# A recurrent vision tower with experts: the token embedding in row halves, its bias added by GpSimd, and another order of the first steps

## The reference

```python
h = patches(x) @ W.T + b                              # 16 x 784 x 64
xp = layernorm(h) @ W_ih.T + b_ih + b_hh
for t in range(16):                                   # the images are the time steps
    hid = tanh(xp[t] + hid @ W_hh.T)
    h2[t] = h[t] + hid
x = layernorm(h2)
top2 = top_k(x @ gate_w + gate_b, 2); w = softmax(top2)
moe = sum over the two of w * (relu(x @ w1[e] + b1[e]) @ w2[e] + b2[e])   # 16 experts, F = 128
y = x + moe
out = h2 + layernorm(y) * gamma + beta
```

## Time and profile before

| | us |
|---|---|
| median of 3 runs | 524.08 |
| the runs | 524.26, 524.08, 521.48 |
| the profiled execution, its own time | 524.21 |
| its span, first to last instruction | 522.4 |
| PE busy | 498.9 (95%) |
| DVE busy | 440.8 (84%) |
| ACT busy | 343.6 (66%) |
| POOL busy | 176.9 (34%) |
| DMA queue q1, share of 16 engines | 56.3% |

### The profile page before, as it was taken

The page is one execution under the profiler, slowest core; times in us unless marked ns, Lnnn a source line. Parts: engine busy times, 40 slices in busy tenths (PEclk is TensorE's granted clock), DMA queues, the critical chain, the costliest instruction groups (busy, mean ns, idle before and its releaser), DMA issues.

```text
span 522.4 us, 8674 instructions
## 1 busy us (share of the span) xinstructions
PE 498.9 (95%) x2943; PEld 331.1 (63%) x2943; DVE 440.8 (84%) x873; ACT 343.6 (66%) x592; POOL 176.9 (34%) x126
## 2 busy tenths in 40 slices
PE   4788999999999999999999999999999999999993
PEld 4464666666666767666666666667666667656552
DVE  1656796998989899898989899898989979999775
ACT  3545575757768585766858576675858577665652
POOL 4220111613325262533425262323516243313233
PEclk9998999999999999999999999999999999999997
DMA  6219076764829185573919377390948548392901
GB/s 139 75 45 232 31 165 140 171 150 109 194 62 230 54 194 124 130 172 85 234 28 221 97 154 168 89 212 25 218 100 181 125 95 193 97 209 65 221 20 32
DMA packets 29755, 69.04 MB, mean 132 GB/s; under 512 B 6432, under 2 KB 8464, under 8 KB 29584
## 3 DMA queue, kind: packets, MB, share of 16 engines
q1 hardware_dynamic: 29712, 68.49, 56.3%
HBM read 60.39 MB, written 8.08 MB: 131 GB/s over the span
## 4 chain that ended last, share of the span: by engine, by line
PE 89%; issue 3%; POOL 3%; DMA 2%; DVE 2%; ACT 1%; POOLq 0%; SPq 0%; DVEq 0%; ACTq 0%
PE pZ L865 37%; PE pO L881 35%; PE pA L780 3%; PE pA L816 2%; PE pA L834 2%; PE pA L895 2%; PE pB L780 2%; PE pA L804 2%; DMA spread<-gates_dram 1%; POOL inv_std L354 1%; PE pB L846 1%; PE pA L792 1%; PE pB L895 1%; PE pB L834 1%; PE pA L805 1%
## 5 line engine op out<-in xcount | busy, mean ns | idle before, releaser
L480 ACT ACTIVATE hexp<-pZ,b1c 128x784 f32<-128x784 f32 x256 | 221.4, 911 | 107.2 <-PE pZ L865 107.2
L881 PE MATMUL pO<-hexp,w2s 128*64 128x392 f32 x1024 | 199.8, 506 | 0.6 <-ACT hexp L480 0.3
L865 PE MATMUL pZ<-xt,w1hi 128*128 128x392 f32 x512 | 189.4, 370 | 1.0 <-ACT xt L411 1.0
L648 DVE SCALAR_TENSOR_TENSOR prod<-pO,b2c,spread 128x392 f32<-128x392 f32 x256 | 150.2, 621 | 44.1 <-PE pO L881 39.5
L865 PE MATMUL pZ<-xt,w1lo 128*128 128x392 f32 x512 | 175.9, 344 | 0.0
L354 POOL TENSOR_TENSOR inv_std<-var,nhalf 112x7 f32<-112x7 f32 x48 | 81.5, 1706 | 183.3 <-DVE var L549 183.3
L865 PEld LDWEIGHTS pZ<-xt,w1hi 128*128 128x128 f32 x512 | 97.3, 190 | 46.5 <-issue 26.3
L881 PEld LDWEIGHTS pO<-hexp,w2s 128*64 128x64 f32 x1024 | 70.5, 136 | 76.0 <-issue 64.9
L664 DVE TENSOR_TENSOR acc<-acc,prod 128x784 f32<-128x784 f32 x111 | 112.2, 1010 | 0.1
L865 PEld LDWEIGHTS pZ<-xt,w1lo 128*128 128x128 f32 x512 | 97.7, 191 | 0.0
L361 POOL TENSOR_TENSOR h2b<-h2c,bet 112x448 f32<-112x448 f32 x15 | 21.5, 1431 | 140.7 <-DMA h2c<-h_dram 140.7
(11 more groups left out here) (103 smaller groups left out, 482.8 us busy)
## 6 DMA issues: line engine op xcount, KB each, us to landing
spread<-gates_dram SPq DMA_DIRECT2D x128, 392.0 KB, 9.0
h_dram<-h SPq DMA_DIRECT2D x16, 248.1 KB, 2.4
h2c<-h_dram SPq DMA_DIRECT2D x16, 248.1 KB, 7.6
xcur<-x_in SPq DMA_DIRECT2D x16, 196.0 KB, 7.6
out<-yo SPq DMA_DIRECT2D x15, 196.0 KB, 7.2
w1f<-w SPq DMA_DIRECT2D x2, 512.0 KB, 6.0
w2s<-w SPq DMA_DIRECT2D x1, 512.0 KB, 3.7
gates_dram<-gt SPq DMA_DIRECT2D x16, 28.0 KB, 2.0
```

The costliest lines, as they stand in the source:

```text
L480: nc.scalar.activation(hexp[u % RING][:, :].rearrange("p (b c) -> p b c", b=2), halves(pZ[u % 2]), ACT.Relu, bias=b1c[:, u:u + 1]).then_in ...
L648: nc.vector.scalar_tensor_tensor(out=prod[q % RING][:, b * HALF:(b + 1) * HALF], in0=halves(pO)[:, b, :], scalar=b2c[:, q:q + 1], in1=spre ...
L865: last = nc.tensor.matmul(halves(pZ[e % 2])[:, b, :], w[:, e, :], xt[par][:, b * HALF:(b + 1) * HALF], start=(k == 0), stop=(k == 1))
L881: last = nc.tensor.matmul(halves(pO)[k * D:(k + 1) * D, b, :], w2s[:, e, :], hexp[e % RING][:, b * HALF:(b + 1) * HALF], start=True, stop= ...
```

## The change

Four things are changed.

1. The embedding. xcur becomes 128 partitions by 448: the even tiles' patches in partitions 0 to 63, the odd tiles' in 64 to 127 (the host orders x so). Each load of x is two transfers. tokw is held twice, once in each half, without the bias row, and embed_in takes rows 0 to 63 for even tiles and 64 to 127 for odd ones. The row of ones and its two fills by GpSimd go.
2. The bias. One more product in the fill makes tokb, the bias spread over 112 partitions, which VectorE copies. From step 3 on, keep_h1 still copies on ScalarE, and a new operation bias_h1 on GpSimd adds tokb in place, between add_beta and the MIX rstd in its queue; the square of h1 waits for it and moves from u = 11 (12 in step 0) to 13, its reduction on VectorE from u = 13 to 14. For steps 0 to 2 VectorE does copy and addition together.
3. Products on zeros: keep_busy(n) issues n products of 128 x 128 with 512 columns into a part of pO that nothing reads: 6 at the start, 9 behind embed_in(0), 4 behind recur(0), 10 ahead of x2_turn(0). VectorE fills their operand first.
4. The order of the fill and of step 0: embed_in(1) moves behind embed_turn(0), hidden_turn(0) ahead of embed_turn(1), gates_turn(0) ahead of first_layer(0, 0) and into another bank (pO), low_part(0) behind find_second(0), and w1's low parts, norms and squares of the first steps change places; in step 0 recur(2) is at u = 5, x2_turn(1) at 7, x2's scaling at 3 and low_part(1) at 5. The spread of step 0's gates is ten transfers instead of eight: the first pair alone, with a semaphore of its own.

The core of the diff:

```diff
-        tokw = sb("tokw", [K_IN + 1, W])
+        tokw = sb("tokw", [2 * D, W])
+        tokb = sb("tokb", [P, W])
-        xcur = [sb(f"xcur{i}", [K_IN + 1, TOK]) for i in range(2)]
+        xcur = [sb(f"xcur{i}", [2 * D, FIRST]) for i in range(2)]
...
+        def gates_turned_in(s):
+            return pO if known(s, 1) else pB
...
-                sp.dma_start(xcur[s % 2][0:K_IN, :], x_in[:, bass.ds(s * TOK, TOK)]).then_inc(xload[s % 2], 16)
+                for k, (first, n) in enumerate(((0, FIRST), (FIRST, REST))):
+                    sp.dma_start(xcur[s % 2][k * D:(k + 1) * D, 0:n],
+                                 x_in[:, bass.ds(s * TOK + first, n)]).then_inc(xload[s % 2], 16)
...
-                for part in range(PARTS):
+                pieces = [(part * (Q // PARTS), Q // PARTS, spread_in[part]) for part in range(PARTS)]
+                if known(s, 1):
+                    pieces[0:1] = [(0, 1, first_spread), (1, Q // PARTS - 1, spread_in[0])]
+                for q0, n, landed in pieces:
...
+            def bias_h1(s, par):
+
+                pool.wait_ge(h1_kept, 2 * s + 2)
+                nc.gpsimd.tensor_tensor(h1[par][:, :, :], h1[par][:, :, :], over_tiles(tokb[:, :], W), ALU.add)\
+                    .then_inc(h1_biased, 1)
...
                 if close:
                     add_beta(t - 1)
+                if embed:
+                    bias_h1(t + 3, 1 - par)
                 if mix:
                     rstd(MIX, t + 2, 1)
...
-                    if gate and u == at(t, 1, first=5):
+                    if gate and u == at(t, 1, first=7):
                         keep_xt(t + 1, 1 - par)
...
-                    if mix and u == at(t, 5, first=7):
+                    if mix and u == 5:
                         new_hidden(t + 2)
...
-                    if embed and u == at(t, 11, first=12):
+                    if embed and u == 13:
                         square_h1(t + 3, 1 - par)
...
+            def keep_h1(s, par):
+
+                dve.wait_ge(h1_made, s + 1)
+                if not known(s, 2):
+                    STATE.wait(dve, s - 2, "h2")
+                for some, n, fresh in zip(some_tiles, (PAIRS, TILES - PAIRS), embedded_in(s)):
+                    nc.vector.tensor_tensor(h1[par][:, some, :], fresh, tokb[:, :].unsqueeze(1).to_broadcast([P, n, W]),
+                                            ALU.add).then_inc(h1_kept, 1)
...
-                    if embed and u == 13:
+                    if embed and u == 14:
                         norm_var(EMBED, a, 0)
...
+            def keep_busy(n):
+
+                for _ in range(n):
+                    nc.tensor.matmul(pO[:, 512:1024], busy[:, 0:128], busy[:, :], start=True, stop=True)
...
-                    last = nc.tensor.matmul(embedded_in(s)[i % 2][:, i // 2, :], xcur[s % 2][:, i * P:(i + 1) * P],
-                                            tokw[:, :], start=True, stop=True)
+                    rows = slice((i % 2) * D, (i % 2 + 1) * D)
+                    last = nc.tensor.matmul(embedded_in(s)[i % 2][:, i // 2, :],
+                                            xcur[s % 2][rows, (i // 2) * P:(i // 2 + 1) * P], tokw[rows, :],
+                                            start=True, stop=True)
...
             embed_in(0)
-            embed_in(1)
+            keep_busy(9)
             pe.wait_ge(consts, IDENT_SET)
             embed_turn(0)
+            embed_in(1)
             pe.wait_ge(cell_loaded, CELL_LOADED)
             recur(0)
+            keep_busy(4)
+            hidden_turn(0)
             embed_turn(1)
-            hidden_turn(0)
             recur(1)
             embed_in(2)
...
+            keep_busy(10)
             x2_turn(0)
+            gates_turn(0, True)
             first_layer(0, 0, 0)
-            gates_turn(0, True)
             first_layer(0, 1, 0)
```

115 lines of the change are left out of this document (65 added, 50 removed).

## The result

The changed kernel took 517.29 us (median of 4 runs, 515.39 to 517.55), the kernel before 524.03 beside it: a ratio of 0.9875, 95% interval 0.9836 to 0.9913. That is 6.7 us or 1.25% less, more than the 0.5% that a measurement of this kernel can tell from no change. The forecast was 518.2, and the measured time lies in its own range (516.5 to 520.5). The profiled execution took 517.41 us, its span is 515.3.

A forecast was written before the change was run, and what follows sets the result against it. The prediction took TensorE, busy 60.00 of 60 us, to bound the kernel. 524.2 less 6.0 in the loop plus 0 for the fill gave 518.2 us, own range 516.5 to 520.5, 8 in 10 from 514.5 to 521.8.

The forecast's parts named there:

- Part 1: Loop, embed_in by row halves: a block takes 0.94 us instead of 1.40, 13 blocks, 6.0 us saved.
- The 9.1 us: Loop, embed_in: upper bound of the saving, if a block took half of 1.40 us; the sum would be 515.1.
- Part 2: Loop, bias on GpSimd: 2.2 us an operation, 0.8 us of VectorE, cost on the path 0.
- Part 3: Fill up to the first residual sum: VectorE waits for the expert weights, add_state(0) at about 22.5, 2.2 us late.
- Part 4: Fill, add_state(0) to gate copy: net 0.3 us worse, bounds -1.4 and +1.8; copy done at about 35.7.
- the 1.3: Fill, up to the gates: us gained by low_part, exp and gates_turn moving, if TensorE is free.
- Part 5: Fill, first pair spread alone: lands in 4.9 us, 2.9 us better; first product at 43.1.
- Part 6: Fill, first product to third pair: 7.6 us, reaching 50.7, plus 0.6 us for a possible cold clock.
- (a): Rival, fill: the zeros work, TensorE at full level at x2_turn(0) and after the pause; 515.5 us, chance 0.22.
- (b): Rival, fill loses: embed_in(1) and all zeros at half clock, the pause cold; 521.4 us, chance 0.15.
- (c): Rival, loop: halves don't overlap, or another engine takes up what TensorE gives; 524.2 us, chance 0.08.
- (d): Rival, loop: GpSimd's bias delays the next state's normalisation; at 1 us over, 531.2 us, chance 0.05.

The follow-up runs named there:

- e2: The changed kernel without GpSimd's addition of the bias to h1 from step 3 on: 516.45 us.
- e5: The changed kernel with SP's five expert weight loads issued ahead of the x loads of steps 2 and 3: 513.07 us.
- e3: The changed kernel without the ten zero products ahead of x2_turn(0): 515.57 us.
- e7: The changed kernel with the first spread in one piece of eight experts' pairs again: 520.69 us.
- e8: The kernel before with only the row halves, two x loads and GpSimd bias; fill in old order, no zero products, spread undivided: 518.43 us.
- e4: The changed kernel without any of the zero products at the start (6, 9, 4 and 10): 517.09 us.
- e6: The changed kernel with 20 more zero products ahead of embed_turn(1) and 4 more behind it: 515.93 us.
- e13: The changed kernel with expert loads ahead of later x loads, seven zeros before and two behind embed_turn(1), eight instead of ten before x2_turn(0): 512.94 us.
- e1: The changed kernel with all seven embedding products of a step on the same 64 partitions, 0 to 63, instead of alternating halves: 527.53 us.

## Why the prediction was right, step by step

**Part 1, the halves.** Right: 0.94 us a block, 13 blocks. The step became shorter by 0.50, not 0.46; the other 0.04 is what small differences of other blocks, up to 0.05 either way, leave, and the loop gave 6.3 where 6.0 were forecast. The argument by the neighbouring block of the same shape carried because it contained the block's end. My remark that the trace disagrees with the Trainium skill (TensorEngine Tiling (Array Packing), Theoretical Speedup) was put too broadly. The factor of up to two holds for the pace of the tiles, 0.196 to 0.098; what it doesn't hold for is the block, whose end isn't halved but grows from 0.15 to 0.29 us. The 9.1 us were wrong because they halved that end too.

**Part 2, the bias on GpSimd.** Right: 1.67 us in the step shown and 1.74 on average (taken 2.2), 3.17 us of cover left behind it where I had 2.8, cost 0 in the step (e2: 0.8 in all by the medians, not clear of noise). The surcharge on VectorE was not where I put it: the sum at 204.41 ran beside L372 and took 0.96. It came at xn instead, 1.56 us where it had been 0.62, with or without the bias (e2), and TensorE had cover for it.

**Part 3, the wait for the expert weights.** Right in kind and nearly in size: w2 sum at 20.81 (21.4), add_state(0) at 21.95 (22.5), 1.65 us late where I had 2.2. The last load landed 2.7 us behind its issue, not 3.3. e5 shows that this wait was the largest single cost in the fill, worth more than its own length.

**Part 4, the gates.** This term was mis-sized, with the right sign: 1.6 us worse than before (14.46 from add_state(0) to the end of the gate copy, before 12.84) where I had 0.3. The reorder itself gains 1.07 (e3: 11.23 to the start of the copy, before 12.30), near the 1.3. The zeros cost the copy 2.7 (13.94 against 11.23) instead of 1.6: they ended 11.6 us behind add_state(0) instead of 11.0, at the low level throughout, and the way from there to the end of the copy took 2.8 us instead of 2.1, with x2_turn(0) still begun at that level. As add_state(0) itself was 0.55 earlier than forecast, the copy was done at 36.41 instead of 35.7.

**Part 5, the first pair.** Right: 4.5 us from issue to product (4.9, between bounds of 3.9 and 5.9; no row stands behind the 5.9). Against the 7.8 of before that is 3.3 us, where I had 2.9; by e7, 2.3 of it is the pair's, since the undivided piece too came sooner in the new fill (6.9). It makes up for the gate copy, 3.3 us later than before (36.41, 33.14): first product at 43.44, forecast 43.1, before 43.46.

**Part 6.** 7.40 us to the third pair (7.6), at 50.84 (50.7). The 0.6 us held for a cold product after the pause wasn't needed: eight records took 1.66 at 45.65. Nor was there the one pause of 2.6 us that I had forecast: TensorE stood still twice for 1.09 us, ahead of 41.40 and of 50.02, where before it was 2.51 ahead of 45.21. What decides between 1.66 and e8's 2.88 was not tested apart, and a pause alone doesn't: in e7 TensorE stood still for 2.43 us ahead of 52.13, and the product behind it, at 52.95, took 1.54; in every kernel with the new order the second pair's product ran at the upper level, in both with the old order at the lower one.

**The sum.** Fill 0 forecast, -0.5 measured; loop -6.0 forecast, -6.3 measured. 518.2 against 517.41 in the profiled execution. The loop's part was reasoned and came as reasoned. That the fill came out so near was in part luck: the gates cost 1.3 us more than I had, and this was made up by four misses the other way, of 0.55 (part 3), 0.4 (part 5), 0.2 and the unneeded 0.6 (part 6).

**The rivals.** (a) is out for the ten: they ran at the low level for 4.63 us. Its other half, the upper level after the pause, came true (1.66 at 45.65). The rule named there (the Trainium skill, TensorE: Matmul & The Clock Gate, What's actually happening) is borne out in the first part of the fill, where the first fifteen zeros brought embed_turn(0) to 0.57 us from 0.98 (e4 without zeros, and the earlier trace rows), and by the profiled executions of e6 (up to 34 us) and e13; it didn't give its time because the clock was lost in the pause ahead of the ten. (b) was there in the late gate copy, and was paid for by the pair's landing and by the pause that wasn't cold. (c) is out by the block of 0.94 us and the step of 29.48; e1 shows that the alternation makes them. (d) is out by the 3.17 us left.

## What to carry to other kernels

Price an edit by the nearest block of the same shape, from its first product to the first of the next block: the end belongs to it, and a factor on the pace applies only to the rest. When a transfer's issue waits for an engine, look at what stands behind it in that queue; here small loads of weights behind a load of later data cost 4 us, over twice what the wait for them showed. Zero products helped by about 1 us where TensorE would have stood still early in the fill (e4 against e3), and cost about as much where they stood ahead of work that was ready (e3); once the expert weights came early, zeros in the gaps moved no median by anything that can be told.

## What the runs showed of the hardware

- A block of 64-row products hands over to a 128-row product later than a block of 65-row products does, 0.29 against 0.15 us (e1, before; 0.29 with alternating halves too). I had not expected that 64 rows on one side would lose 0.13 us a block to 65.
- Operations of VectorE and GpSimd on SBUF hold each other up, and the phase seems to decide who pays. Of the kernel before:

```profile
220.45 1.67 POOL L369 TENSOR_TENSOR yn<-yn,gam 112x448 f32<-112x448 f32 x1 [0.65 <-ACT yn L427]
220.49 0.62 DVE L560 TENSOR_TENSOR xn<-h,inv_std 112x448 f32<-112x448 f32 x1
```

Now xn starts at 216.91, 0.25 us behind a GpSimd multiplication of 1.32 us, and takes 1.56, ending 0.5 us behind it; before, it started 0.04 us behind such an operation and took 0.62 (the mean 618 ns), while GpSimd's took 1.67 instead of 1.32. GpSimd's last addition fell from 1867 ns to 1364 on average, as xn rose to 1325. The sum at 204.41 had begun before L372 and took its usual 0.96. That a late starter is held to the end of the other, not slowed in proportion, agrees with the Trainium skill (SBUF — State Buffer, SBUF: two separate sides), which speaks of an exclusive lock for the whole instruction; that xn of before, which started 0.04 us after GpSimd's, was not held is not explained by it.
- The same load, issued at 18.07 to 18.13, landed 2.7 us later in the changed kernel and 4.1 in e6. Executions of one kernel differ by 0.4 us (e3) to 4.0 us (e7: 518.12 to 522.10), while from kernel to kernel the part behind the third pair is the same to 0.5 us in the traces with row halves on both sides.
- The profile lists a granted clock of 1.00 until its first change: in e4 it says 1.00 from 30 to 36 us, while x2_turn's four products at 32.21 took 1.01 us, as they did in e3 at a listed 0.50. In the fill I went by the durations.
